# One-hots of two slots per compare, and a four-slot ring that is handed over by pairs

## The chip, the cores and the metric

The kernel runs on one core of a Trainium2 chip. The time is device time in microseconds (us). A core has five engines with their own instruction streams: PE (TensorE, matmuls; its weight loads are listed as PEld), DVE (VectorE), ACT (ScalarE), POOL (GpSimd) and SP (SyncE, which issues most of the DMAs). They meet only at semaphores: an instruction raises one when it is done, and an engine stands at a wait until a semaphore has reached a value.

## The reference

A graph of 6250 nodes with 128 features and 200000 edges that are sorted by destination. Two layers, each added to its input and normalised. What the part under change needs is the sum over a node's edges of the features of the edge's source:

```python
h = node_features @ W + b_W
xi, xj = jnp.split(h, 2, axis=-1)
xji = xj[senders] + (edge_features @ W_e + b_We)
in_degree = jax.ops.segment_sum(jnp.ones_like(receivers), receivers, num_segments=num_nodes)
nodes = xi + jax.ops.segment_sum(xji / (in_degree[receivers] + 1e-06), receivers, num_segments=num_nodes)
x = _layernorm(x + nodes)
...
out = jax.ops.segment_sum(h[src] * norm[:, None], dst, num_segments=N) + b   # second layer, same edges
```

## The kernel before

No row of x is gathered edge by edge. Nodes are cut into NB = 25 blocks of 256 destinations. For each block the kernel counts how often each source node occurs among the edges of each destination (a matrix of counts), and the sum over edges is then a matrix product of x, split in two 16-bit parts, with these counts.

**Counts.** The destinations of a block are taken two by two; eight such windows of up to 128 edges are a *slot*. A block has SL = 16 slots (the last block 7). For a slot VectorE makes two one-hot arrays out of small tables, `lo_oh` (low part of the source's number, 1024 elements per partition) and `key_oh` (high part and which of the two destinations, 800 elements): function `one_hots(b, s)`, lines 594 and 597. TensorE multiplies them, eight matmuls (`count(b, s)`, line 828), and ScalarE copies the result out of PSUM into `counts` (`pair_out`, line 1035).

**The ring.** `lo_oh` and `key_oh` hold RING = 4 slots. VectorE waits before slot number `at` until the semaphore `built` has reached `at + 1 - RING`, that is until slot `at - 4` has been counted. Each slot's second compare raises `hot` by one; TensorE's `count` waits for `hot >= at + 1`. ScalarE's `tables(b)` waits for `hot` too, before it overwrites the tables from two blocks back.

**The order.** Each engine runs a loop over blocks b and slots s that is written out by hand; nothing schedules it. TensorE in block b: at each slot `count(b, s)`, and from slot 1 on a share of `product(b - 1, s)` (lines 846 and 854, the products with the counts of the block before: 98 of them and up to 48 more for the second layer, spread over 15 slots, so 7 to 10 a slot); at slot 1 `messages`, at slot 3 `turn_keys(b + 1)` (line 881), at slots 5 and 11 the edge features' sums `edges` (line 865, 72 matmuls each). VectorE in block b: at each slot `one_hots(b, s)`, and behind it at slot 1 `count_heads` (541), at slot 2 `make_keys(b + 1)` (561 to 581) and `edge_keys(b - 1)` (606), at slot 3 `edge_one_hots(b - 1, 0)` (614) and `z_low` (699), at slot 6 `offset`, at 7 `invert_degrees` and `sums`, at 8 and 9 `count_row` and `start_of`, at 10 the second `edge_one_hots`, at 12 `normalise`. GpSimd's `check_edges` (491 to 494) follows `edge_keys`. Some 700 us in, all blocks are counted; then comes the second layer's gather (line 911), with the counts loaded again, and the normalisation, which use no one-hots.

Of the kernel before, what the change touches and what calls it, by code (L numbers as in the profile page):

```python
# [23 lines left out]
ALU = mybir.AluOpType  # L24
# [3 lines left out]
P = 128  # L28
# [3 lines left out]
NB = -(-N // BN)  # L32
# [3 lines left out]
KW = 2 * HI  # L36
WE = 128
SW = 8
SL = 16
RING = 4  # L40
# [37 lines left out]
def slots(b):  # L78
    return SL if b < NB - 1 else LAST_SLOTS


def first_slot(b):
    return SL * b


def cols(b):
# [60 lines left out]
def reach(engine, sem, value):  # L147


    if not isinstance(value, int) or value > 0:  # L150
        engine.wait_ge(sem, value)
# [43 lines left out]
def layers(nc, block, x, src, dst, ea, W0, b0, We, be, keep, scratch):  # L195
    with ExitStack() as ctx:
# [8 lines left out]
        lo_oh = sb("lo_oh", [P, RING, SW // 2, P, 2], BF16)  # L205
# [10 lines left out]
        key_oh = sb("key_oh", [P, RING, SW // 2, KW, 2], BF16)  # L216
        counter = sb("counter", [P, P, 2], BF16)
# [18 lines left out]
        key_t, lo_t = ([sb(f"{n}{i}", [P, P], BF16) for i in range(2)] for n in ("key_t", "lo_t"))  # L236
# [295 lines left out]
        def _(dve):  # L532
            dv = nc.vector
# [53 lines left out]
            def one_hots(b, s):  # L587
                if s == 0:
                    dve.wait_ge(S["tabled"], b + 1)
                at = first_slot(b) + s  # L590
                reach(dve, S["built"], at + 1 - RING)
                w = slice(SW * s, SW * (s + 1))
                pairs = lambda a: a.rearrange("p (w t) -> p w t", t=2).unsqueeze(2)
                dv.tensor_tensor(lo_oh[:, at % RING, :, :, :],  # L594
                                 counter[:, :, :].unsqueeze(1).to_broadcast([P, SW // 2, P, 2]),
                                 pairs(lo_t[b % 2][:, w]).to_broadcast([P, SW // 2, P, 2]), ALU.is_equal)
                dv.tensor_tensor(key_oh[:, at % RING, :, :, :],  # L597
                                 counter[:, 0:KW, :].unsqueeze(1).to_broadcast([P, SW // 2, KW, 2]),
                                 pairs(key_t[b % 2][:, w]).to_broadcast([P, SW // 2, KW, 2]), ALU.is_equal)\
                  .then_inc(S["hot"], 1)  # L600

            def edge_keys(b):
# [25 lines left out]
            def scales():  # L628
                dve.wait_ge(S["few_out"], 1)
                step(dv.tensor_reduce(out=top[:, :], in_=few_ps[0:1, 0, 0:P], axis=AX.X, op=ALU.max))  # L630
                dv.tensor_scalar(expo[:, :], top[:, :].bitcast(I32), EXP_BITS, None, ALU.bitwise_and)
                few_f = few[:, :].bitcast(F32)
                dv.tensor_scalar(few_f[:, 2:3], top[:, :], ROW_LEAST, None, ALU.mult)
                dv.tensor_scalar(few_f[:, 3:4], top[:, :], X_LEAST, None, ALU.is_ge)
                step(dv.tensor_scalar(sound[:, :], top[:, :], X_MOST, None, ALU.is_le))
                dv.tensor_scalar(few[:, 0:1], expo[:, :], -1.0, float((2 * 127 + X_TOP) * ONE_EXP), ALU.mult, ALU.add)
                dv.tensor_scalar(few[:, 1:2], expo[:, :], -float(X_TOP * ONE_EXP), None, ALU.add)
                step(dv.tensor_tensor(few_f[:, 3:4], few_f[:, 3:4], sound[:, :], ALU.mult))
                dve.sem_inc(S["few_ready"], 1)
# [51 lines left out]
            def normalise(u):  # L691
                dve.wait_ge(S["std_ready"], u + 1)
                dv.reciprocal(std[:, :], std[:, :]).then_inc(S["scale_known"], 1)
# [30 lines left out]
            for b in range(NB + 2):  # L724
                u = b - 2
                for s in range(SL):
                    if b < NB and s < slots(b):
                        one_hots(b, s)
                    if b == 0:
                        if s == 0:  # L730
                            scales()
                        if s == 1:
                            spread_scales()
                        if s == 3:
                            invert_degrees(0)
                    if SL * b + s in LOW_AT:
                        split_low(LOW_AT.index(SL * b + s))
                    if s == 1 and b + 3 < NB:
                        count_heads(b + 3)
                    if s == 2 and b + 1 < NB:  # L740
                        make_keys(b + 1)
                    if b == 1 and s == 6:
                        ready_weights()
                    if s == 2 and 1 <= b < NB:
                        edge_keys(b - 1)
                    if s == 3 and 1 <= b < NB:
                        edge_one_hots(b - 1, 0)
                    if s == (7 if b else 10) and b + 1 < NB:
                        invert_degrees(b + 1)
                    if s == 6 and 0 <= u < NB:  # L750
                        offset(u)
                    if s == 7 and 0 <= u < NB:
                        sums(u)
                    if s == 4 and b == 0:
                        count_row(2)
                    if s == 5 and b == 0:
                        start_of(2)
                    if s == 8 and b + 3 < NB:
                        count_row(b + 3)
                    if s == 9 and b + 3 < NB:  # L760
                        start_of(b + 3)
                    if s == 12 and 0 <= u < NB:
                        normalise(u)
                    if s == (10 if b < NB - 1 else 4) and 1 <= b < NB:
                        edge_one_hots(b - 1, 1)
                    if s == 8 and b == NB - 1:
                        edge_keys(b)
                        edge_one_hots(b, 0)
                    if s == 3 and 1 <= u <= NB:
                        z_low(u - 1)  # L770
# [50 lines left out]
        def _(pe):  # L821
            def count(b, s):
                at = first_slot(b) + s
                pe.wait_ge(S["hot"], at + 1)
                reach(pe, S["pair_out"], at - 1)
                for w in range(SW):
                    half_of, col = w // 4, (w % 4) * KW
                    last = nc.tensor.matmul(pair_ps[at % 2][:, half_of, col:col + KW],  # L828
                                            lo_oh[:, at % RING, w // 2, :, w % 2], key_oh[:, at % RING, w // 2, :, w % 2],
                                            start=True, stop=True)  # L830
                last.then_inc(S["built"], 1)
# [188 lines left out]
        def _(act):  # L1020
# [34 lines left out]
            def tables(b):  # L1055
                act.wait_ge(S["turned"], b + 1)
                if b >= 2:
                    act.wait_ge(S["hot"], first_slot(b - 1))
                a.copy(key_t[b % 2][:, :], keys_ps[:, 0, :])
                a.copy(lo_t[b % 2][:, :], keys_ps[:, 1, :]).then_inc(S["tabled"], 1)  # L1060

# [714 lines left out]
```

## Time and profile before

| | |
|---|---|
| median of 3 runs | 942.07 us (940.08 to 942.12) |
| span of the profiled execution | 940.7 us |
| mean granted TensorE clock | 0.983 of full speed |
| busy: PE, DVE, ACT, POOL | 95%, 74%, 48%, 45% |
| matmuls of `count` (L828) | 3128 |
| compares of `lo_oh`, of `key_oh` | 391 each |

The page gives busy shares for the whole span, which mixes the block loop (to some 700 us) with the second layer (from there on, where VectorE has little to do). Busy times by stretch, the list of waits and the timeline tell the stages apart. A timeline row has the start in us from the span's start, the duration, engine, line, operation, tile written and tiles read, shape, how many instructions are merged into the row, and in brackets how long the engine was idle just before and what ended that.

### The profile page before, as it was taken

What the parts mean: (1) busy time and instruction counts of PE and PEld (TensorE: products, weight loads), DVE (VectorE), ACT (ScalarE), POOL (GpSimd) and SP (SyncE); (2) the same over time, 40 slices, a digit from 0 to 9 for tenths busy, and PEclk for the clock granted to TensorE, in tenths of its full rate; (3) what the DMA queues carried; (4) which work ended last, traced back from release to release, by engine and by line L of the source; (5) the groups of instructions that cost most, each with busy time, mean ns of one, the idle gap of its engine ahead of it and who ended that gap; (6) DMA issues with size and microseconds to landing.
All of it is one profiled execution on the core that took longest, in us unless ns stands there. A gap on an engine that the chain in (4) does not pass through costs nothing.

```text
span 940.7 us, 30861 instructions
## 1 busy us (share of the span) xinstructions
PE 890.2 (95%) x12193; PEld 794.2 (84%) x12193; DVE 695.5 (74%) x1636; ACT 454.9 (48%) x962; POOL 419.3 (45%) x498
## 2 busy tenths in 40 slices
PE   5679999999999999999999999999999999999995
PEld 4667888888988998989999999999988888888864
DVE  5898999999999998898888899888842111112255
ACT  3765665566656665565565556565542000000035
POOL 3347557555764555655565575544332011111100
PEclk9689999999999999999999999999999999999998
DMA  5475888899797987777687777688767887779635
GB/s 164 132 232 212 314 289 293 313 325 315 263 324 286 316 304 236 266 218 248 244 284 249 236 250 211 243 281 258 231 207 305 341 346 285 270 259 324 248 123 165
DMA packets 95727, 244.82 MB, mean 260 GB/s; under 512 B 41194, under 2 KB 63400, under 8 KB 89688
## 3 DMA queue, kind: packets, MB, share of 16 engines
q1 hardware_dynamic: 92312, 237.49, 72.5%
q0 software_dynamic: 2400, 4.88, 1.6%
q8 instruction: 100, 1.64, 0.7%
q10 hardware_dynamic: 864, 0.39, 0.2%
q14 instruction: 51, 0.42, 0.1%
HBM read 183.88 MB, written 58.85 MB: 258 GB/s over the span
## 4 chain that ended last, share of the span: by engine, by line
PE 81%; DVE 10%; issue 3%; ACT 2%; DMA 2%; POOL 0%; ACTq 0%; DVEq 0%
PE x_ps L846 24%; PE pair_ps L911 17%; PE pair_ps L828 13%; PE e_ps L865 10%; PE x_ps L854 9%; DVE key_oh L597 3%; DVE lo_oh L594 3%; PE j_ps L893 2%; DMA early_in<-sums_z 1%; PE pair_ps L920 1%; PE j_ps L894 1%; PE u_vps L1379 1%; ACT counts L1035 1%; DMA xsplit<-in_dst 1%; PE j_ps L943 1%
## 5 line engine op out<-in xcount | busy, mean ns | idle before, releaser
L1035 ACT CAST counts<-pair_ps 128x784 bf16<-128x784 f32 x391 | 315.4, 817 | 256.1 <-PE pair_ps L828 255.3
L846 PE MATMUL x_ps<-counts,xsplit 128*128 128x256 bf16 (+1 forms) x2450 | 306.1, 271 | 1.2 <-issue 1.2
L594 DVE TENSOR_TENSOR lo_oh<-counter,lo_t 128x1024 bf16<-128x1024 bf16 x391 | 274.4, 702 | 41.7 <-PE pair_ps L828 39.8
L846 PEld LDWEIGHTS x_ps<-counts,xsplit 128*128 128x128 f16 x2450 | 221.1, 98 | 31.4 <-issue 9.8
L597 DVE TENSOR_TENSOR key_oh<-counter,key_t 128x800 bf16<-128x800 bf16 x391 | 232.7, 595 | 0.0
L828 PE MATMUL pair_ps<-key_oh,lo_oh 128*128 128x100 bf16 x3128 | 208.5, 209 | 12.9 <-DVE key_oh L597 7.2
L828 PEld LDWEIGHTS pair_ps<-key_oh,lo_oh 128*128 128x128 bf16 x3128 | 182.9, 98 | 27.9 <-DVE key_oh L597 10.9
L865 PE MATMUL e_ps<-streams 128*32 128x128 f32 x3528 | 106.6, 274 | 0.0
L854 PE MATMUL x_ps<-counts,zown 128*128 128x256 bf16 (+1 forms) x840 | 105.9, 269 | 0.6 <-issue 0.6
L911 PE MATMUL pair_ps<-streams,zown 128*128 128x256 bf16 x878 | 99.0, 273 | 0.0
L865 PEld LDWEIGHTS e_ps<-streams 128*32 128x32 f32 x3528 | 93.4, 110 | 4.8 <-issue 1.0
L911 PEld LDWEIGHTS pair_ps<-streams,zown 128*128 128x128 f16 x878 | 85.8, 98 | 11.4 <-issue 0.2
L1184 ACT ACTIVATE xsplit<-xsplit,vec 128x256 f32<-128x256 f32 (+1 forms) x25 | 12.6, 503 | 154.6 <-DVE xsplit L803 154.6
L468 POOL TENSOR_SCALAR bias<-linear,share 128x128 f32<-128x128 f32 x50 | 80.0, 1604 | 14.8 <-DVE vo L680 13.9
L854 PEld LDWEIGHTS x_ps<-counts,zown 128*128 128x128 f16 x840 | 76.1, 97 | 10.9 <-issue 3.4
L911 PE MATMUL pair_ps<-counts,zown 128*128 128x256 bf16 (+1 forms) x732 | 79.9, 269 | 0.0
L911 PEld LDWEIGHTS pair_ps<-counts,zown 128*128 128x128 f16 x732 | 69.3, 98 | 9.2
L436 POOL TENSOR_SCALAR row_f<-cnt 128x1 f32<-128x1 f32 x25 | 14.6, 586 | 121.2 <-DVE head_junk L541 121.1
L614 DVE TENSOR_TENSOR streams<-iota,ekeys 128x1152 f32<-128x1152 f32 x49 | 66.3, 1354 | 0.1
L431 POOL DMA_INDIRECT gsrc<-in_src,start_i x25 | 62.6, 2506 | 7.6 <-issue 7.6
L795 DVE TENSOR_TENSOR s_mem<-pair_ps,early_in 128x256 f32<-128x256 f32 (+1 forms) x23 | 9.6, 418 | 72.6 <-PE pair_ps L911 69.4
L483 POOL TENSOR_TENSOR streams<-streams,key_oh 128x512 bf16<-128x512 bf16 x13 | 15.0, 1150 | 91.0 <-DMA streams<-counts_kept 91.0
(179 smaller groups left out, 881.1 us busy)
## 6 DMA issues: line engine op xcount, KB each, us to landing
streams<-in_edge_attr SPq DMA_DIRECT2D x196, 576.0 KB
counts_kept<-counts SPq DMA_DIRECT2D x10, 1600.0 KB, 9.2
streams<-counts_kept SPq DMA_DIRECT2D x6, 1600.0 KB, 6.5
counts<-counts_kept SPq DMA_DIRECT2D x4, 1600.0 KB, 6.5
counts_kept<-counts SPq DMA_DIRECT2D x2, 3136.0 KB, 12.1
streams<-counts_kept SPq DMA_DIRECT2D x2, 3136.0 KB, 14.6
edst<-in_dst SPq DMA_DIRECT2D x196, 4.5 KB, 1.9
counts<-in_x SPq DMA_DIRECT2D x3, 1024.0 KB, 8.9
```

Source lines behind the costliest of these rows:

```text
L431: g.indirect_dma_start(out=out, out_offset=None, in_=table, in_offset=bass.IndirectOffsetOnAxis(ap=at, axis=0)).then_inc(done, 16)
L468: last = g.tensor_scalar(bias[:, t, :], bje, share[:, 2 * b + t:2 * b + t + 1], None, ALU.mult)
L594: dv.tensor_tensor(lo_oh[:, at % RING, :, :, :], counter[:, :, :].unsqueeze(1).to_broadcast([P, SW // 2, P, 2]), pairs(lo_t[b % 2][:, w]). ...
L597: dv.tensor_tensor(key_oh[:, at % RING, :, :, :], counter[:, 0:KW, :].unsqueeze(1).to_broadcast([P, SW // 2, KW, 2]), pairs(key_t[b % 2][: ...
L614: dv.tensor_tensor(e_oh[g][:, :, :], iota[:, 0:EC].unsqueeze(1).to_broadcast([P, EG * EJ, EC]), ekeys[:, k].unsqueeze(2).to_broadcast([P, ...
L828: last = nc.tensor.matmul(pair_ps[at % 2][:, half_of, col:col + KW], lo_oh[:, at % RING, w // 2, :, w % 2], key_oh[:, at % RING, w // 2, : ...
L846: last = nc.tensor.matmul(x_ps[:, 0, 0:n], xsplit[:, q // 2, q % 2, :], by_hi[:, q // 2, :], start=(q == 0), stop=(q == 2 * HS - 1))
L854: last = nc.tensor.matmul(x_ps[:, 1, 0:n], zsplit[:, z // 2, z % 2, :], by_hi[:, z // 2, :], start=(z == 0), stop=(z == early(k) - 1))
L865: last = nc.tensor.matmul(e_ps[EC * c:EC * (c + 1), g, :], e_oh[g][:, c * EJ + j, :], ebuf[g][:, c, j, :], start=(j == 0), stop=(j == EJ - 1))
L893: nc.tensor.matmul(out, sx[:, t:m:2], wj, start=True, stop=False)
L911: last = nc.tensor.matmul(z_ps[i % 2][:, 0:n], zsplit[:, q // 2, q % 2, :], by_hi[:, q // 2, :], start=(q == early(b)), stop=(q == 2 * HS ...
L1035: a.copy(out.rearrange("p h (g n) -> p h g n", g=2), pair_ps[at % 2][:, :, 0:4 * KW].rearrange("p g (n h) -> p h g n", h=HI)[:, 0:HS]).the ...
```

## The change

One call of `one_hots` makes the one-hots of two slots (of one, where a block has an odd slot left: only the last block's seventh). It is called at even slots. Its two compares have 2048 and 1600 elements per partition. It waits until the later of the two slots that it overwrites has been counted, and raises `hot` once for the pair, so the waits for `hot` count pairs.

```diff
+def hot_pairs(at):
+    return -(-at // 2)
...
             def one_hots(b, s):
                 if s == 0:
                     dve.wait_ge(S["tabled"], b + 1)
-                at = first_slot(b) + s
-                reach(dve, S["built"], at + 1 - RING)
-                w = slice(SW * s, SW * (s + 1))
+                at, n = first_slot(b) + s, min(2, slots(b) - s)
+                reach(dve, S["built"], at + n - RING)
+                w, g = slice(SW * s, SW * (s + n)), SW // 2 * n
+                ring = slice(at % RING, at % RING + n)
                 pairs = lambda a: a.rearrange("p (w t) -> p w t", t=2).unsqueeze(2)
-                dv.tensor_tensor(lo_oh[:, at % RING, :, :, :],
-                                 counter[:, :, :].unsqueeze(1).to_broadcast([P, SW // 2, P, 2]),
-                                 pairs(lo_t[b % 2][:, w]).to_broadcast([P, SW // 2, P, 2]), ALU.is_equal)
-                dv.tensor_tensor(key_oh[:, at % RING, :, :, :],
-                                 counter[:, 0:KW, :].unsqueeze(1).to_broadcast([P, SW // 2, KW, 2]),
-                                 pairs(key_t[b % 2][:, w]).to_broadcast([P, SW // 2, KW, 2]), ALU.is_equal)\
+                dv.tensor_tensor(lo_oh[:, ring, :, :, :].rearrange("p r w k t -> p (r w) k t"),
+                                 counter[:, :, :].unsqueeze(1).to_broadcast([P, g, P, 2]),
+                                 pairs(lo_t[b % 2][:, w]).to_broadcast([P, g, P, 2]), ALU.is_equal)
+                dv.tensor_tensor(key_oh[:, ring, :, :, :].rearrange("p r w k t -> p (r w) k t"),
+                                 counter[:, 0:KW, :].unsqueeze(1).to_broadcast([P, g, KW, 2]),
+                                 pairs(key_t[b % 2][:, w]).to_broadcast([P, g, KW, 2]), ALU.is_equal)\
                   .then_inc(S["hot"], 1)
...
-                    if b < NB and s < slots(b):
+                    if b < NB and s < slots(b) and s % 2 == 0:
                         one_hots(b, s)
...
-                pe.wait_ge(S["hot"], at + 1)
+                pe.wait_ge(S["hot"], hot_pairs(at + 1))
...
-                    act.wait_ge(S["hot"], first_slot(b - 1))
+                    act.wait_ge(S["hot"], hot_pairs(first_slot(b - 1)))
```

VectorE's order in a block of the loop's middle, from slot 2 to slot 5, before. L594 and L597 are a slot's two compares, L561 to L581 `make_keys` (its middle is left out), L606 `edge_keys`, L614 `edge_one_hots`, L699 `z_low`; the brackets name the semaphores waited for:

```order
L594 TENSOR_TENSOR lo_oh<-counter,lo_t 128x1024 [waits built]
L597 TENSOR_TENSOR key_oh<-counter,key_t 128x800
L561 TENSOR_SCALAR bit_i<-gsrc 128x128 [waits turned,window_in0]
...
L606 TENSOR_TENSOR ekeys<-edst,ebase 128x72 [waits e_checked,edge_dst_in0]
L594 TENSOR_TENSOR lo_oh<-counter,lo_t 128x1024 [waits built]
L597 TENSOR_TENSOR key_oh<-counter,key_t 128x800
L614 TENSOR_TENSOR streams<-iota,ekeys 128x1152 [waits e_keyed,e_summed]
L699 SCALAR_TENSOR_TENSOR zown<-x_mem,zscale,zown 128x128 [waits z_high,x1_ready]
L699 SCALAR_TENSOR_TENSOR zown<-x_mem,zscale,zown 128x128
L594 TENSOR_TENSOR lo_oh<-counter,lo_t 128x1024 [waits built]
L597 TENSOR_TENSOR key_oh<-counter,key_t 128x800
L594 TENSOR_TENSOR lo_oh<-counter,lo_t 128x1024 [waits built]
```

The same place after (line numbers have moved by 4 or 5; L599 and L602 are the compares of two slots):

```order
L599 TENSOR_TENSOR lo_oh<-counter,lo_t 128x2048 [waits built]
L602 TENSOR_TENSOR key_oh<-counter,key_t 128x1600
L565 TENSOR_SCALAR bit_i<-gsrc 128x128 [waits turned,window_in0]
...
L611 TENSOR_TENSOR ekeys<-edst,ebase 128x72 [waits e_checked,edge_dst_in0]
L619 TENSOR_TENSOR streams<-iota,ekeys 128x1152 [waits e_keyed,e_summed]
L704 SCALAR_TENSOR_TENSOR zown<-x_mem,zscale,zown 128x128 [waits z_high,x1_ready]
L704 SCALAR_TENSOR_TENSOR zown<-x_mem,zscale,zown 128x128
L599 TENSOR_TENSOR lo_oh<-counter,lo_t 128x2048 [waits built]
L602 TENSOR_TENSOR key_oh<-counter,key_t 128x1600
```

Slot 3's compares have moved from behind `edge_keys` to ahead of `make_keys`, and slot 5's stand in one with slot 4's. Between the pair of slots 2 and 3 and that of slots 4 and 5 now lies all the other work of slots 2 and 3 in one piece.

## Rows read from the trace of the kernel before

**Rows 1.** The page, busy us (share of the span) and instructions of each engine.

```profile
PE 890.2 (95%) x12193; PEld 794.2 (84%) x12193; DVE 695.5 (74%) x1636; ACT 454.9 (48%) x962; POOL 419.3 (45%) x498
```

**Rows 2.** Busy us by stretch: PE, PEld, DVE, ACT, POOL; clock, DMA share, GB/s.

```profile
120.00:160.00 40.00, 37.89 (x658) 33.78 (x659) 40.00 (x93) 23.62 (x47) 23.67 (x26) 1.00 0.81 274
440.00:480.00 40.00, 39.97 (x662) 36.50 (x658) 37.36 (x87) 22.59 (x44) 27.62 (x26) 1.00 0.78 256
```

**Rows 3.** Waits: who waited for whom, us in total, times, longest us.

```profile
POOL row_f L436 <- DVE head_junk L541: 121.1, 23, 8.8
...
DVE lo_oh L594 <- PE pair_ps L828: 39.8, 47, 2.7
...
PE pair_ps L828 <- DVE key_oh L597: 7.2, 10, 1.7
```

**Rows 4.** Timeline of DVE, block 15, from slot 0 to slot 6.

```profile
426.70 0.69 DVE L594 TENSOR_TENSOR lo_oh<-counter,lo_t 128x1024 bf16<-128x1024 bf16 x1 [2.15 <-PE pair_ps L828]
...
429.18 0.31 DVE L541 TENSOR_SCALAR_CACHE_REDUCE head_junk<-heads_sb,th 128x98 bf16<-128x98 f32 x1
...
429.54 0.69 DVE L594 TENSOR_TENSOR lo_oh<-counter,lo_t 128x1024 bf16<-128x1024 bf16 x1
...
430.63 0.22 DVE L561 TENSOR_SCALAR bit_i<-gsrc 128x128 int32<-128x128 int32 x1
...
432.54 0.68 DVE L594 TENSOR_TENSOR lo_oh<-counter,lo_t 128x1024 bf16<-128x1024 bf16 x1
433.14 0.57 DVE L597 TENSOR_TENSOR key_oh<-counter,key_t 128x800 bf16<-128x800 bf16 x1
433.62 1.35 DVE L614 TENSOR_TENSOR streams<-iota,ekeys 128x1152 f32<-128x1152 f32 x1
434.89 0.60 DVE L699 SCALAR_TENSOR_TENSOR zown<-x_mem,zscale,zown 128x128 f16<-128x128 f32 x2
435.42 0.82 DVE L594 TENSOR_TENSOR lo_oh<-counter,lo_t 128x1024 bf16<-128x1024 bf16 x1
...
437.92 0.68 DVE L594 TENSOR_TENSOR lo_oh<-counter,lo_t 128x1024 bf16<-128x1024 bf16 x1
```

**Rows 5.** Timeline of PE: slot 15 of block 14 and slot 4 of block 15.

```profile
430.67 0.53 PE L828 MATMUL pair_ps<-key_oh,lo_oh 128*128 128x100 bf16 x8
...
437.91 0.53 PE L828 MATMUL pair_ps<-key_oh,lo_oh 128*128 128x100 bf16 x8
```

**Rows 6.** Timeline of POOL at the same place: `check_edges`, its first addition.

```profile
435.32 0.37 POOL L492 TENSOR_TENSOR eacc<-eacc,ein 128x72 f32<-128x72 f32 x1
```

**Rows 7.** Timeline, block 4: slot 4's second compare, the next instruction, slot 4's count.

```profile
145.35 0.61 DVE L597 TENSOR_TENSOR key_oh<-counter,key_t 128x800 bf16<-128x800 bf16 x1
145.88 0.82 DVE L594 TENSOR_TENSOR lo_oh<-counter,lo_t 128x1024 bf16<-128x1024 bf16 x1
146.02 0.54 PE L828 MATMUL pair_ps<-key_oh,lo_oh 128*128 128x100 bf16 x8 [0.86 <-DVE key_oh L597]
```

**Rows 8.** Timeline of PE: slot 15 before blocks 3, 7, 10, and slot 4.

```profile
113.17 0.53 PE L828 MATMUL pair_ps<-key_oh,lo_oh 128*128 128x100 bf16 x8
...
120.79 0.54 PE L828 MATMUL pair_ps<-key_oh,lo_oh 128*128 128x100 bf16 x8 [1.20 <-DVE key_oh L597]
...
216.86 0.53 PE L828 MATMUL pair_ps<-key_oh,lo_oh 128*128 128x100 bf16 x8
...
223.45 0.53 PE L828 MATMUL pair_ps<-key_oh,lo_oh 128*128 128x100 bf16 x8
...
294.44 0.88 PE L828 MATMUL pair_ps<-key_oh,lo_oh 128*128 128x100 bf16 x16
...
301.34 0.53 PE L828 MATMUL pair_ps<-key_oh,lo_oh 128*128 128x100 bf16 x8
```

**Rows 9.** Busy us by stretch in block 1, columns as in rows 2.

```profile
63.00:66.00 3.00, 1.41 (x17) 1.08 (x17) 3.00 (x6) 1.02 (x2) 2.79 (x5) 1.00 0.91 393
66.00:70.00 4.00, 3.24 (x35) 2.67 (x39) 3.96 (x8) 1.35 (x4) 1.37 (x3) 0.57 0.79 330
```

## The prediction

> **What bounds the kernel now.** I read the page's engine line first: TensorE is busy 95% of the span, VectorE 74% [rows 1]. That is a mean over stages, so the next view was the busy time by stretch. In 440 to 480 us TensorE is busy 39.97 of 40 us and VectorE 37.4; in 120 to 160 us it is the other way round, VectorE 40.00 and TensorE 37.9 [rows 2]. So the block loop has a front part in which VectorE decides and a long rest in which TensorE does. The list of waits gives the size: in the whole run TensorE's count matmuls (L828) waited for a one-hot ten times, 7.2 us in total, while VectorE waited 47 times, 39.8 us, for a buffer that the counts had not yet freed [rows 3]. So at most 7.2 us can be had by making one-hots sooner, and VectorE has idle time nearly everywhere. What the change can lose is in how that idle time lies: TensorE is fed only because VectorE runs ahead of it into four slot buffers.
>
> **The compares.** In block 15, at slot 3, the compare of the low part takes 0.60 us to the start of the next instruction, that of the keys 0.48 [rows 4]. For 1024 and 800 elements that is 0.536 ns an element and some 0.05 us that doesn't scale. A merged pair of slots therefore costs 2.16 - 2 x 0.05 = 2.06 us instead of 2.16. The 391 slots (24 blocks of 16, the last of 7) become 196 pairs, so VectorE loses about 195 x 0.10 = 20 us of work. The bounds of the saving are 0 and, from the full durations 0.68 and 0.57 in the same rows (slope 0.49 ns, rest 0.18 to 0.19 where they don't overlap), 0.37 us a pair; I take 0.10, since the instructions follow each other here with the overlap that the start times show. This saving reaches the end only where TensorE waited for a one-hot.
>
> A page speaks for the change. The Trainium skill, "VectorE: DVE Perf Modes", section "Rules for kernel authors", says to keep the number of VectorE instructions low, and "Vector Engine (DVE) Microarchitecture Reference", section 5.2, puts about 75 ns on each. By that a pair would cost 2.01 us and the forecast below would be about 2 us lower; the start times here give 50 ns.
>
> **The ring.** This is the term that decides. One-hots have four slot buffers. Before, slot n may be written when slot n-4 has been counted. After, pair (n, n+1) may be written when slot n-3 has been counted, the later of the two it overwrites. And in VectorE's order the second slot of a pair moves ahead of the work that stood between the two: in every block the order at slots 2 to 5 becomes pair (2,3), then make_keys and edge_keys, the edge one-hots, z_low, then pair (4,5). Before, slot 3's compares stood between edge_keys and the edge one-hots.
>
> Follow block 15. TensorE counts slot 15 of block 14 from 430.67 to 431.20 and starts on slot 4 of block 15 at 437.91, 6.71 us later [rows 5]. Pair (2,3) overwrites slots 14 and 15 of block 14, so it can't start before 431.20. (Pair (0,1) is gated by slot 13; VectorE today waits there too, 2.15 us [rows 4], and it and the 0.36 us of count_heads are done in time.) From 431.20 VectorE has to do, before TensorE can start on slot 4:
> - one semaphore step, 0.06 us, and pair (2,3), 2.06;
> - make_keys and edge_keys, 430.63 to 432.54: 1.91 [rows 4];
> - the edge one-hots, 433.62 to 434.89: 1.27 [rows 4];
> - z_low, 434.89 to 435.42: 0.53 [rows 4];
> - pair (4,5), 2.06, and what GpSimd adds. Today the four compares of slots 4 and 5 take 435.42 to 437.92, 2.50 [rows 4], 0.34 over the undisturbed 2.16, and the first of them coincides with GpSimd's L492 [rows 6]. That work follows edge_keys, so it falls on pair (4,5) again. Between 0 and 0.34 I take 0.17;
> - 0.14 from the next instruction's place on VectorE to TensorE's start, as in block 4: 145.88 to 146.02, where TensorE did wait for this compare [rows 7].
>
> Sum: 0.06 + 2.06 + 1.91 + 1.27 + 0.53 + 2.06 + 0.17 + 0.14 = 8.20 us. TensorE is there after 6.71, so it stands 1.49 us. The stall returns each block: the next slot 15 is counted 1.49 later, and so is its chain's start. Nothing hides it, since TensorE is the full engine there and its order is fixed. After slot 4 the other pairs are in time: pair (6,7) follows (4,5) at once and is used two slots and 2.1 us of edges later; continued in the same way, the walk has pair (10,11) and the second edge one-hots done over 1 us before TensorE wants them.
>
> On GpSimd's share a page and a row differ. The row shows 0.82 for a compare that takes 0.68 elsewhere, so 0.14 for an overlap of 0.27 us (L492 from 435.32, 0.37 long) [rows 4, 6]. The Trainium skill, "SBUF — State Buffer", section "SBUF: two separate sides", has the two engines share a port as an exclusive lock for a whole instruction. By that pair (4,5) would wait 0.3 to 0.7 us and the sum would be 3 to 12 us higher; the trace shows half an overlap, and I go by it.
>
> **The other blocks.** What a block gains in length is 8.20 minus its time from the end of slot 15 to the start of slot 4 today, whatever stall that time already holds. The 12 blocks 12 to 23 have ten products a slot and look like block 15: 12 x 1.49 = 17.9. Blocks 8 to 11 have nine: in block 10 it is 294.97 (0.53 into a row of 16) to 301.34, 6.37 [rows 8], so 4 x 1.83 = 7.3. Blocks 6 and 7, eight: 217.39 to 223.45, 6.06 [rows 8], 2 x 2.14 = 4.3. Blocks 3 to 5 are like block 3: 113.70 to 120.79, 7.09, of which 1.20 is already a wait for the one-hot [rows 8]: 3 x 1.11 = 3.3. Block 2 has block 3's products without its wait, 5.89: 2.3. Block 1 has today two waits at slots 3 and 4 and no z_low; its chain comes out within 0.3 us, taken as 0.2. In block 0 the first count waits for two slots instead of one, 2.06 - 1.08, about 1.0, and scales() moves by as much. Block 24 has no make_keys and edge work before slot 4: 0. Smaller waits for one-hots in blocks 2 to 5, some 0.8 us of the 7.2, go: -0.8.
>
> Total: 17.9 + 7.3 + 4.3 + 3.3 + 2.3 + 0.2 + 1.0 - 0.8 = 35.5 us. Hidden at no cost: count_heads, sums, count_row and start_of come up to one pair later, and their users (GpSimd's row_of, ScalarE's root, the gathers for two blocks on) have several us; deg_known comes some 2.6 us later for GpSimd, which waits 121 us for count_heads alone today [rows 3]. ScalarE's tables(b) waits for the same one-hots as before, counted in pairs. The second phase from 700 us on has no one-hots and only moves.
>
> The profiled execution has a span of 940.7 us; the median of the three runs is 942.07, 1.4 above. 942.1 + 35.5 = 977.6, rounded to 977.
>
> **Rivals.**
> 1. *Faster: the ring still covers.* If pair (4,5) came within 6.7 us of slot 15's count, only the saving would be left, and TensorE would get back what it waited for VectorE, at most 7.2 us [rows 3]: 935. For it speaks VectorE's large idle time. It decides where the chain drops below TensorE's 6.71 us; for that 1.5 us of 8.20 must go, and the largest saving per pair that a row allows, 0.37, takes 2 x 0.27. I give it 5%. It is also what the rule on instruction counts would give.
> 2. *Nothing to see.* The saving in the front part and stalls of 0.2 to 0.3 us a block cancel: 942. 3%.
> 3. *Half the stall.* Compares cheaper than I take them (2 x 0.27) and no GpSimd share, so a chain of 7.5: 0.7 less in each of the 22 blocks 2 to 23, 15 us off, 962. 9%.
> 4. *The clock falls too.* In block 1 TensorE stood twice for one-hots, was busy 1.41 of 3.0 us, and the granted clock was 0.57 in the next 4 us, the lower of its two levels (1.2 instead of 2.4 GHz) for most of it [rows 9]. That costs up to 4 x 0.43 = 1.7 us. A single wait of 1.20 in block 3 had no such fall. The new stalls are 1.5 to 2.3 us. Falls in blocks 2, 6 and 7 alone add 5 us, inside my range; in all 22 blocks 37 us: 1015. 8% for more than a third of the blocks.
> 5. *The change doesn't do what it says*, the merged compare running at a lower rate than two: each 1 us on a pair would add 2 us to every chain, near 1020. Shape and types are the same but for the count of groups. 2%.
>
> **How the numbers follow.** My case has 73%. Its range is set by the chain: without GpSimd's share and with 0.15 less a pair it is 7.7 us, 11 us less over the 22 blocks; without any saving and with all of 0.34 it is 8.57, 8 more; blocks 0 to 2 may add or take 2. So 966 to 988, which leaves out rivals 1 to 3 and most of 4 and 5. A difference of 0.3%, 2.8 us, is about what a measurement of this kernel can tell from none. Faster by more: 5%. Within: 3%. Slower by more: 92%.
>
> **What the changed profile would show.** TensorE's L828 waiting for key_oh some 23 times, once a block at slot 4, 35 to 40 us in total instead of 7.2; VectorE waiting for L828 at about three places a block; blocks 15 to 23 with a period 1.5 us longer; a merged low compare of about 1.15 us and a merged key compare of 0.91 to the next start; the granted clock at 1.00 through the loop. I am wrong if L828's waits stay under 15 us, if they lie at other slots than 4, or if the merged compares take other than 2.0 to 2.2 us together.

## The result and the profile after

The changed kernel takes 990.37 us (median of 6 runs, 989.92 to 993.55) beside 942.1 us of the kernel before on the same chip: ratio 1.051, 95% interval 1.0483 to 1.0537. The forecast was 977 us with a range of 966 to 988. Sign, place and mechanism of the main loss came as forecast; the time is 13 us above the forecast and 2.4 us above the range, because two losses beside it had no term in the sum. The profiled execution has a span of 988.0 us, 47.3 more than the 940.7 before, and it is these 47.3 us that are accounted for below.

The page of after, busy us by engine; it answers to [rows 1]:

```profile
PE 896.9 (91%) x12193; PEld 794.2 (80%) x12193; DVE 674.0 (68%) x1246; ACT 453.4 (46%) x962; POOL 428.3 (43%) x498
```

VectorE has 390 instructions and 21.5 us of work less, and TensorE the same instructions and a smaller share. The saving is real and buys nothing. The waits of after (us in total, times, longest), to be read beside [rows 3]:

```profile
POOL row_f L440 <- DVE head_junk L545: 176.3, 23, 11.5
...
DVE lo_oh L599 <- PE pair_ps L833: 103.9, 65, 3.9
...
PE pair_ps L833 <- DVE key_oh L602: 44.4, 29, 2.5
```

TensorE waits 44.4 us for one-hots instead of 7.2, VectorE 103.9 us for a free buffer instead of 39.8: each engine waits for the other in turn. By stretch (columns as in [rows 2]) TensorE has lost its full 40 us in the steady part, and in the front part the clock is no longer 1.00:

```profile
120.00:160.00 40.00, 35.12 (x540) 30.68 (x539) 34.27 (x61) 19.23 (x40) 27.11 (x31) 0.91 0.78 270
440.00:480.00 40.00, 38.50 (x604) 34.85 (x605) 33.63 (x60) 21.85 (x43) 22.44 (x26) 1.00 0.81 264
```

**The chain in one block.** This is the timeline of after from slot 15 of block 15 to slot 4 of block 16, the block after the one of [rows 4] and [rows 5]. First TensorE, then VectorE.

```profile
458.65 0.53 PE L833 MATMUL pair_ps<-key_oh,lo_oh 128*128 128x100 bf16 x8
...
467.52 0.54 PE L833 MATMUL pair_ps<-key_oh,lo_oh 128*128 128x100 bf16 x8 [1.47 <-DVE key_oh L602]
```

```profile
459.21 1.23 DVE L599 TENSOR_TENSOR lo_oh<-counter,lo_t 128x2048 bf16<-128x2048 bf16 x1 [0.71 <-PE pair_ps L833]
460.36 0.98 DVE L602 TENSOR_TENSOR key_oh<-counter,key_t 128x1600 bf16<-128x1600 bf16 x1
461.26 0.22 DVE L565 TENSOR_SCALAR bit_i<-gsrc 128x128 int32<-128x128 int32 x1
...
463.02 0.23 DVE L611 TENSOR_TENSOR ekeys<-edst,ebase 128x72 f32<-128x72 int32 x1
463.35 1.36 DVE L619 TENSOR_TENSOR streams<-iota,ekeys 128x1152 f32<-128x1152 f32 x1
464.63 0.61 DVE L704 SCALAR_TENSOR_TENSOR zown<-x_mem,zscale,zown 128x128 f16<-128x128 f32 x2
465.15 1.36 DVE L599 TENSOR_TENSOR lo_oh<-counter,lo_t 128x2048 bf16<-128x2048 bf16 x1
466.44 1.02 DVE L602 TENSOR_TENSOR key_oh<-counter,key_t 128x1600 bf16<-128x1600 bf16 x1
467.38 1.35 DVE L599 TENSOR_TENSOR lo_oh<-counter,lo_t 128x2048 bf16<-128x2048 bf16 x1
```

Slot 15 is counted at 459.18. VectorE, idle 0.71 us for just that, starts pair (2,3) at 459.21 and works without a pause until pair (4,5) is done; TensorE starts slot 4 at 467.52. That is 8.34 us, forecast 8.20. Before, TensorE took 6.71 [rows 5], so the block grows by 1.63 us, and it does so in each of blocks 12 to 22.

**Where the 47.3 us are**, by comparing the start of each slot's count matmuls in the two traces, from one slot to the next:
- slot 4 of blocks 2 to 23: 37.7 us;
- slots 5 and 6 of blocks 3, 4 and 7, right behind that stall, at the lower clock: 4.7 us;
- slots 8 to 12 of seven blocks (4, 11, 12, 18, 19, 21, 22), where TensorE waits for no one-hot: 6.5 us;
- gone: 0.8 us of small waits at slot 11 of blocks 2, 3 and 5, and 1.1 us of other gaps that the trace of before has in blocks 5, 6 and 9;
- blocks 0 and 1 together: 0.1 us.

That makes 47.1; the rest is rounding and the part behind the loop.

### The profile page after: what moved, and what is told of

The parts are those of the page before. It is cut to its first block, busy times and chain, and to the rows that moved or that the text cites. A ratio compares the mean times of both kernels' runs of the same rounds, so it can differ in the third digit from the quotient of the medians.

```text
span 988.0 us, 30471 instructions
## 1 busy us (share of the span) xinstructions
PE 896.9 (91%) x12193; PEld 794.2 (80%) x12193; DVE 674.0 (68%) x1246; ACT 453.4 (46%) x962; POOL 428.3 (43%) x498
## 3 DMA queue, kind: packets, MB, share of 16 engines
q8 instruction: 100, 1.64, 0.7%
## 4 chain that ended last, share of the span: by engine, by line
PE 70%; DVE 16%; issue 8%; DMA 2%; ACT 2%; POOL 0%; DVEq 0%; ACTq 0%
PE x_ps L851 19%; PE pair_ps L916 16%; PE pair_ps L833 12%; PE e_ps L870 11%; PE x_ps L859 8%; DVE key_oh L602 5%; DVE lo_oh L599 4%; DMA early_in<-sums_z 1%; PE pair_ps L925 1%; DVE zown L704 1%; PE u_vps L1384 1%; ACT counts L1040 1%; PE j_ps L948 1%; DMA rows<-in_dst,row_i 1%; PE e_ps L878 1%
## 5 line engine op out<-in xcount | busy, mean ns | idle before, releaser
L599 DVE TENSOR_TENSOR lo_oh<-counter,lo_t 128x2048 bf16<-128x2048 bf16 x196 | 248.2, 1267 | 105.8 <-PE pair_ps L833 103.9
L833 PE MATMUL pair_ps<-key_oh,lo_oh 128*128 128x100 bf16 x3128 | 208.8, 209 | 52.3 <-DVE key_oh L602 44.4
L602 DVE TENSOR_TENSOR key_oh<-counter,key_t 128x1600 bf16<-128x1600 bf16 x196 | 200.9, 1025 | 0.0
L870 PE MATMUL e_ps<-streams 128*32 128x128 f32 x3528 | 109.2, 278 | 0.7 <-issue 0.7
L870 PEld LDWEIGHTS e_ps<-streams 128*32 128x32 f32 x3528 | 95.4, 112 | 6.3 <-issue 1.9
L472 POOL TENSOR_SCALAR bias<-linear,share 128x128 f32<-128x128 f32 x50 | 70.9, 1425 | 11.9 <-DVE vo L685 10.9
L808 DVE TENSOR_TENSOR xsplit<-pair_ps,dinv_row 128x256 f32<-128x256 f32 (+1 forms) x25 | 10.5, 419 | 58.2 <-PE pair_ps L925 57.0
```

The source lines that it names most:

```text
L472: last = g.tensor_scalar(bias[:, t, :], bje, share[:, 2 * b + t:2 * b + t + 1], None, ALU.mult)
L599: dv.tensor_tensor(lo_oh[:, ring, :, :, :].rearrange("p r w k t -> p (r w) k t"), counter[:, :, :].unsqueeze(1).to_broadcast([P, g, P, 2]) ...
L602: dv.tensor_tensor(key_oh[:, ring, :, :, :].rearrange("p r w k t -> p (r w) k t"), counter[:, 0:KW, :].unsqueeze(1).to_broadcast([P, g, KW ...
L870: last = nc.tensor.matmul(e_ps[EC * c:EC * (c + 1), g, :], e_oh[g][:, c * EJ + j, :], ebuf[g][:, c, j, :], start=(j == 0), stop=(j == EJ - 1))
```

## The experiments

Theory A is that of the forecast: pairs over four buffers make VectorE wait for slot 15, and everything between pair (2,3) and pair (4,5) then lies on TensorE's path. Theory B: the merged compare itself is slow. Theory C, formed on the result: the stalls also bring the clock down, which multiplies them. Each kernel was run beside the kernel before (medians 942.3 to 943.0 us); "increment" is what a block gains at slot 4 over the kernel before.

### One part of the change at a time

All three have single compares, one slot each. The first only waits by pairs for the ring:

```
-                reach(dve, S["built"], at + 1 - RING)
+                if s % 2 == 0:
+                    reach(dve, S["built"], at + min(2, slots(b) - s) - RING)
```

> One slot per compare and the old order; only the wait for the ring is by pairs (at even slots, for both slots that are overwritten). Theory A (the new stall is a chain on VectorE that starts when slot 15 is counted: ring wait, order and hand-over by pairs make it long): the chain to slot 4 has one slot's compares less ahead of slot 4 than in the changed kernel, 0.06 + 1.08 + 1.91 + 1.08 + 1.27 + 0.53 + 1.08 + 0.17 + 0.14 = 7.3 us against TensorE's 6.71, so 0.6 us a block at slot 4 and more in the blocks with fewer products: about 956 us (950 to 962). Theory B (the merged compares themselves cost, by their length or by what they block): 942 us.

Measured: 962.73 us, ratio 1.0221 (1.018 to 1.0263). The increment is 0.77 us in blocks 14 to 21, 0.8 to 1.5 in blocks 7 to 13.

The second only has the order of pairs:

```
-                    if b < NB and s < slots(b):
-                        one_hots(b, s)
+                    if b < NB and s < slots(b) and s % 2 == 0:
+                        for k in range(s, min(s + 2, slots(b))):
+                            one_hots(b, k)
```

> One slot per compare, ring wait and hand-over slot by slot; only the order is that of the changed kernel (the compares of slots s and s+1 in a row, the other work behind both). Theory A: only slot 3's compares wait for slot 15, so the chain is 0.06 + 1.08 + 1.91 + 1.27 + 0.53 + 1.08 + 0.17 + 0.14 = 6.2 us, under 6.71: no stall at slot 4 in the blocks with ten products, 942 us (939 to 947). Theory B: 942 us too.

Measured: 945.49 us, ratio 1.0047 (1.0025 to 1.0069). No increment in blocks 12 to 23.

The third has both edits, which is the kernel after without the merging and with one hand-over a slot:

> One slot per compare, with the order and the ring wait of the changed kernel; what is left out of the change is the merging and the hand-over by pairs (TensorE may take slot 4 before slot 5 is made). Theory A: 0.06 + 2.16 + 1.91 + 1.27 + 0.53 + 1.08 + 0.17 + 0.14 = 7.3 us, 0.6 us a block: 956 us (950 to 962); the 1.0 us a block from here to the changed kernel's 8.34 is slot 5's share of pair (4,5). Theory B: 942 us, all of the loss being in the merged compares.

Measured: 967.99 us, ratio 1.0271 (1.0243 to 1.0299); increment 0.82 in blocks 14 to 22. The waits of TensorE for one-hots in the three, in this order:

```profile
PE pair_ps L829 <- DVE key_oh L598: 25.4, 28, 1.7
```
```profile
PE pair_ps L829 <- DVE key_oh L597: 7.1, 8, 1.8
```
```profile
PE pair_ps L830 <- DVE key_oh L598: 23.8, 24, 1.8
```

What follows: waiting by pairs makes a stall by itself, the order by itself costs 2.5 us of time and nothing in blocks 12 to 23. Wait and order give half of the increment of 1.63. I put the other half down to the hand-over, which no run has by itself: with single compares TensorE may start slot 4 when slot 4's one-hots are there, a merged pair is handed over only with slot 5's, about 1 us later, less what merging saves. Both kernels came out above their expected 956, since I had put down only the steady blocks' increment: blocks 7 to 13 grow by up to 1.5 us, and each trace has some 3 to 5 us of gaps at slots 9 to 12 with no wait for VectorE.

### More buffers

The kernel after with six buffers. The third pair's low parts lie in an unused tail of `streams`, its keys in a new tile; a few small tiles share space to make room.

```
-RING = 4
+RING = 6
+KEPT = 4
...
+        key_more = sb("key_more", [P, RING - KEPT, SW // 2, KW, 2], BF16)
```

> The changed kernel with six slot buffers instead of four (the third pair lies in memory that is free in the block loop; a few small tiles share memory for it). Pair (2,3) then waits for slot 13, about 3 us sooner, while merging, order and hand-over by pairs stay. Theory A: the chain reaches slot 4 after some 5.3 us, no stall, TensorE's waits for one-hots fall below 7 us, time 934 to 942. Theory B: the merged compares cost the same as in the changed kernel, 980 to 990 us. Theory C (beyond the chain, clock falls and unexplained gaps in TensorE's stream add some 9 us of their own): if they follow from the stalls they are gone here, if not the time stays some us above 942.

Measured: 940.09 us, ratio 0.996 (0.9937 to 0.9983). No increment in blocks 7 to 23, and TensorE waits for one-hots about as long as before the change:

```profile
PE pair_ps L843 <- DVE key_oh L612: 8.1, 7, 2.5
```

So merged compares cost nothing by themselves and theory B falls; in after, too, a pair's two compares take 1.15 + 0.90 = 2.05 us to the next start (459.21, 460.36 and 461.26 above), forecast 2.06. This kernel is faster than both, by 0.4% over the one before.

### The chain made shorter and longer

Four buffers and pairs as in after; edge_keys and the first edge one-hots are moved ahead of pair (0,1), z_low behind pair (4,5). The first line makes edge_keys wait until VectorE's own earlier edge one-hots are done:

```
+                reach(dve, S["e_hot"], edge_group(b, 0))
...
+                    if s == 0 and 1 <= b < NB:
+                        edge_keys(b - 1)
+                        edge_one_hots(b - 1, 0)
                     if b < NB and s < slots(b) and s % 2 == 0:
                         one_hots(b, s)
...
-                    if s == 3 and 1 <= u <= NB:
+                    if s == 5 and 1 <= u <= NB:
                         z_low(u - 1)
```

> The kernel after, four buffers and pairs as they are; only the work that stands on VectorE between pair (2,3) and pair (4,5) is thinned: edge_keys and the first edge one-hots stand before pair (0,1), z_low behind pair (4,5). Theory A (the stall at slot 4 is the chain from slot 15's count, 8.34 us, minus TensorE's 6.71): the chain loses 1.27 + 0.4 + 0.53 us and is 6.1 to 6.4, below 6.71, so the wait at slot 4 is gone in blocks 12 to 23 and the time is 938 to 948, with some stalls left in blocks 3 to 11. Rival (pairs over four buffers cost a stall wherever the other work stands): 965 to 990.

Measured: 941.47 us, ratio 0.9989 (0.9969 to 1.0009). The increment is 0.00 in blocks 10 to 23. The chain now reads (timeline of VectorE, one block):

```profile
456.06 1.23 DVE L599 TENSOR_TENSOR lo_oh<-counter,lo_t 128x2048 bf16<-128x2048 bf16 x1 [0.71 <-PE pair_ps L833]
...
458.10 0.22 DVE L565 TENSOR_SCALAR bit_i<-gsrc 128x128 int32<-128x128 int32 x1
...
459.86 1.23 DVE L599 TENSOR_TENSOR lo_oh<-counter,lo_t 128x2048 bf16<-128x2048 bf16 x1
461.01 0.98 DVE L602 TENSOR_TENSOR key_oh<-counter,key_t 128x1600 bf16<-128x1600 bf16 x1
461.91 0.60 DVE L705 SCALAR_TENSOR_TENSOR zown<-x_mem,zscale,zown 128x128 f16<-128x128 f32 x2
```

Pair (4,5) is done 5.85 us after pair (2,3) starts (456.06 to 461.91), under TensorE's 6.71. This takes the whole loss back with only the order changed and that wait added, so the loss was the chain.

The opposite: the first edge one-hots of each block written twice, the second time after a wait for the first.

```
-                        edge_one_hots(b - 1, 0)
+                        edge_one_hots(b - 1, 0, 2)
```

> The kernel after, with the first edge one-hots of each block written twice, so that the chain to slot 4 is longer by one compare, 1.27 us, and one wait for itself, about 0.1. Theory A (every us on the chain is a us of the block): +1.4 us in blocks 2 to 23, 30 us, so 1017 to 1024. Theory C (longer waits bring the granted clock down after most of them, at 1.5 us each): in 22 blocks up to 33 us more, 1030 to 1055. If the time stays under 1005, the chain isn't what TensorE waits for.

Measured: 1048.77 us, ratio 1.113 (1.1112 to 1.1149). The increment is 3.12 us in blocks 12 to 22 (3.35 in block 14), 1.49 more than in after: theory A's term. It makes 69.9 us over blocks 2 to 23 instead of 37.7. Another 29.9 us lie at slots 5 and 6, where after has 4.7: the granted clock falls at 17 of these 22 stalls. One of them, by stretch (columns as in [rows 2]):

```profile
450.00:475.00 25.00, 21.18 (x301) 18.77 (x299) 20.23 (x34) 13.50 (x28) 12.86 (x13) 0.99 0.54 185
474.70:478.10 3.40, 3.40 (x38) 2.70 (x39) 3.19 (x7) 1.90 (x4) 1.13 (x4) 0.50 1.16 215
480.00:505.00 25.00, 24.47 (x342) 21.77 (x337) 16.31 (x30) 14.14 (x28) 8.32 (x12) 1.00 0.67 227
```

So theory A and theory C both hold: a us on the chain is a us of the block, and a stall of 3 us or more costs 1.4 to 1.7 us more in most blocks.

### After, a second time

> The kernel after, unchanged, for a second trace. Theory A: the wait at slot 4 is 1.4 to 1.6 us in blocks 12 to 23 again, and the time is 988 to 994. The falls of the granted clock (blocks 3, 4, 7 in the first trace, 4.7 us) and the gaps of TensorE at slots 8 to 12 (about 6 us in the first trace, in blocks 4, 11, 12, 18, 22) lie in the same blocks if the program's order makes them, and elsewhere if they are chance.

Measured: 986.52 us (984.85 to 993.03), ratio 1.0494 (1.0454 to 1.0534); span of this trace 982.8. Slot 4 of blocks 2 to 23 gives 37.7 us, as in the first trace. The clock falls again behind block 3 and block 4 and this time not in block 7 (3.1 us). The gaps at slots 8 to 12 are in part elsewhere (blocks 3, 13 and 14; blocks 4 and 21 have them again; 4.6 us, net of what is gone 1.9). So the stall at slot 4 is fixed by the program; which blocks have gaps and falls of the clock is partly chance. The two traces differ mainly by these, and by 1.2 us in blocks 0 and 1.

### One slot a compare over six buffers

The edit of the six buffers, in the kernel before. It was to part what six buffers gave from what merging gave.

> The kernel before, with six buffers instead of four, one slot a compare as before. It parts what six buffers gave in the pairs' kernel (940.1) from what merging gave. If the one wait that six buffers take away is that of TensorE for one-hots (7.2 us in all before, 2 to 4 of them in blocks 3 to 6), it comes out at 938 to 941, the same as the pairs; if merging gave the gain, at 942 to 944.

Measured: 963.21 us, ratio 1.022 (1.0167 to 1.0273). Both expectations failed. TensorE waits hardly at all for one-hots (4.0 us), but in blocks 10 to 21 slot 6 is 0.9 to 1.7 us late, 14 us in all, since the edge matmuls of slot 5 (72, before 2.17 us) stop in the middle. Timeline of TensorE, then of GpSimd:

```profile
450.68 1.85 PE L877 MATMUL e_ps<-streams 128*32 128x128 f32 x48
452.86 0.89 PE L877 MATMUL e_ps<-streams 128*32 128x128 f32 x24 [0.33 <-issue]
```
```profile
450.79 1.15 POOL L442 DMA_INDIRECT gdst<-in_dst,start_i  x1 [0.27 <-issue]
452.25 3.78 POOL L442 DMA_INDIRECT gsrc<-in_src,start_i  x1 [0.31 <-issue]
```

GpSimd's gathers for a later block wait, through its `shares`, for invert_degrees on VectorE. With six buffers VectorE runs further ahead, and the gathers start 0.1 us into the edges. In the kernel before they start some 0.8 us after the edges, in the six-buffer kernel of pairs mostly 1.2 to 1.9 us after their start. That made theory D: the gathers disturb the edges. The test moves invert_degrees on VectorE:

```
-                    if s == (7 if b else 10) and b + 1 < NB:
+                    if s == 10 and b + 1 < NB:
                         invert_degrees(b + 1)
```

> The kernel with six buffers and one slot a compare (963.2 us), with invert_degrees of the next block moved on VectorE from slot 7 to slot 10. GpSimd's share, and behind it its gathers for a later block, wait for invert_degrees; in that kernel they start in the first us of TensorE's edge matmuls of slot 5, and these took 3.0 us instead of 2.2 in blocks 10 to 21, 1.1 us a block. In the kernel before, the gathers start 0.8 us after the edges end. Theory D (the gathers' start slows the edge matmuls): moved by some 3 us, the gathers come after the edges and the 1.1 us are gone in 12 blocks: 944 to 952. Rival (one slot a compare over six buffers delays something else at slot 5): 958 to 966.

Measured: 959.07 us, ratio 1.0161 (1.0129 to 1.0193). The disturbance is gone: blocks 12 to 22 are as long as in the kernel before, to within 0.07 us, and the idle time inside the edge matmuls (view of that line) falls from the first of these rows to the second:

```profile
  issue: 24.0, 58
```
```profile
  issue: 5.2, 14
```

But the time hardly moved, because the gathers are now late. In blocks 3, 6 and 11 VectorE's make_keys waits for them, and each of these blocks is 6.3 to 6.5 us longer:

```profile
DVE bit_i L572 <- DMA gsrc<-in_src,start_i: 27.7, 5, 7.6
```

So theory D holds as to the coincidence, and a new wait took the gain. Why a gather's start slows those matmuls the trace doesn't say. In blocks 12 to 22 three kernels agree: singles over four buffers, singles over six with this move, and pairs over six. Merging gives the steady part nothing and takes nothing from it.

### Both cures together

Six buffers and the short chain.

> Six buffers, pairs, and the short chain (edge_keys and the first edge one-hots ahead of pair (0,1), z_low behind pair (4,5)). Six buffers alone left TensorE 8 us of waits for one-hots, all in blocks 1 to 6; the short chain alone (four buffers) left 5.8. Theory A: no stall is left in blocks 7 to 23, and the front part may give 2 to 5 us: 934 to 940. If the front part is bound by VectorE's whole work, as its 100% busy share at 120 to 160 us says, the order does nothing: 938 to 942.

Measured: 942.94 us, ratio 1.0006 (0.999 to 1.0022). No gain over six buffers alone, and no better than before. The forecast for theory A missed, but not at the one-hots: slot 4 of blocks 3 to 6 is 3.5 us earlier than in the kernel before (2.5 with six buffers alone), and the 6.1 us of waits that are left lie in blocks 0 and 1. What took the gain is slot 6, which comes 0.2 to 0.6 us late in each of blocks 11 to 22, 3.6 us in all. GpSimd's gathers now start next to the edge matmuls of slot 5, and these take 2.4 to 2.8 us instead of 2.17, theory D's loss in a smaller size. Block 15, TensorE and GpSimd:

```profile
439.34 2.40 PE L881 MATMUL e_ps<-streams 128*32 128x128 f32 x72
```
```profile
438.95 1.46 POOL L446 DMA_INDIRECT gdst<-in_dst,start_i  x1 [0.27 <-issue]
440.72 1.37 POOL L446 DMA_INDIRECT gsrc<-in_src,start_i  x1 [0.30 <-issue]
```

## Why the prediction was right and where it was not

**Right: what decides, and where.** The stall is at slot 4, once a block, from slot 15's count through pair (2,3), make_keys, edge_keys, edge one-hots, z_low and pair (4,5). Shortening that list took the loss away, lengthening it by one compare raised it by 1.49 us a block. TensorE waited 29 times, 44.4 us, where some 23 times and 35 to 40 us were forecast. The saving of 0.10 us a pair is what the trace shows (2.05 against 2.16), and it reaches nothing, as forecast. Rivals 1, 2, 3 and 5 are out: the ring doesn't cover (44.4 us of waits), the increment isn't half, and the compare isn't slow.

**Right, partly by luck: the price of a shared moment with GpSimd.** Pair (4,5) took 2.23 us from 465.15 to 467.38, the 2.06 + 0.17 of the sum, while three GpSimd instructions ran beside it:

```profile
465.05 0.38 POOL L496 TENSOR_TENSOR eacc<-eacc,ein 128x72 f32<-128x72 f32 x1
465.52 1.24 POOL L497 TENSOR_SCALAR ein<-ekeys 128x72 f32<-128x72 f32 x1
466.84 0.81 POOL L498 TENSOR_TENSOR eacc<-eacc,ein 128x72 f32<-128x72 f32 x1
```

The 0.17 was the middle of 0 to 0.34, and nothing in the rows of before chose it. GpSimd paid more than VectorE: the last two of these took 0.71 and 0.40 us in block 15 of the kernel before. The Trainium skill, "SBUF — State Buffer", section "SBUF: two separate sides", has such instructions of the two engines exclude each other from start to end; by the prediction's estimate from that it would have been 2.36 us or more, so the trace doesn't agree here. The Trainium skill, "Vector Engine (DVE) Microarchitecture Reference", section 5.2, gives about 75 ns for an instruction; the two instructions saved per pair gave 0.11 us together, 55 ns each.

**Mis-sized by 0.18 us a block: make_keys and edge_keys.** I took 1.91 us from [rows 4], and it was 2.09 (461.26 to 463.35). The difference is behind edge_keys: it is 0.33 us from its start to the edge one-hots, before it was 0.15 to the next compare, at 432.54 [rows 4]:

```profile
432.39 0.22 DVE L606 TENSOR_TENSOR ekeys<-edst,ebase 128x72 f32<-128x72 int32 x1
```

Before, slot 3's compares stood between the two, so the edge one-hots found their keys ready; now they stand right behind the instruction whose semaphore they wait for. The change moves the cover away, and I priced the steps one by one as if the order between them didn't matter. Against it stand 0.04 us of small overestimates; the chain is 8.34 instead of 8.20. Over the blocks this gives 37.7 us where the sum had 35.1.

**Wrong: rival 4 was a matter of yes or no.** I gave the falling clock 8% as a case of its own and left it out of the forecast, though the text says that falls in blocks 2, 6 and 7 would add 5 us. It fell in blocks 3, 4 and 7 and added 4.7. It belonged into the sum: the trace of before shows a fall in block 1 [rows 9], and from the sum, with the waits that were there already, stalls of 1.8 to 2.3 us followed for blocks 2 to 7. The rows after block 3's stall and after block 7's (columns as in [rows 2]):

```profile
121.00:124.40 3.40, 0.96 (x15) 0.66 (x13) 3.40 (x6) 0.90 (x2) 3.08 (x6) 1.00 0.33 90
124.40:127.80 3.40, 3.40 (x44) 2.77 (x45) 3.38 (x7) 1.96 (x4) 1.92 (x4) 0.50 1.00 218
127.80:131.20 3.40, 3.40 (x77) 3.04 (x70) 1.94 (x6) 0.26 (x1) 2.83 (x3) 0.99 0.60 234
205.00:208.40 3.40, 1.30 (x17) 0.96 (x16) 3.40 (x4) 1.32 (x3) 3.15 (x4) 1.00 0.22 43
234.00:237.10 3.10, 1.40 (x20) 1.32 (x21) 3.10 (x4) 0.82 (x2) 1.75 (x2) 0.99 0.30 71
237.10:240.50 3.40, 3.40 (x65) 3.04 (x65) 3.38 (x7) 1.14 (x3) 1.78 (x4) 0.50 1.06 206
```

In the second row TensorE is busy all the time at 0.50, the lower level of 1.2 GHz; in the third the clock is back. The fourth row is block 6: a stall of 2.11 us, as long as block 7's, and no fall. "The clock at 1.00 through the loop" was wrong for three stretches.

**Wrong: no term for what comes and goes.** The sum put the gaps at slots 8 to 12 at nothing; they are 6.5 us in the first trace and 4.6 in the second. All but those at slot 12 follow a signal of TensorE that arrives late (last section). In blocks 2 to 23 the trace of before has one such signal that is over 0.6 us late, each trace of after eight, so the change may bring them; by what step isn't shown. The trace of before also has two gaps of the kind at slot 12, 0.57 and 1.24 us in blocks 5 and 6, which I had not looked at, since they lie far from any wait on VectorE. The gaps are part of why single executions of after lie between 985 and 994 us. The range had 2 us for "blocks 0 to 2" and nothing for this.

**Blocks 0 and 1** were put at 1.2 us and gave 0.1. The small waits for one-hots that go gave the 0.8 us forecast. In sum 35.5 became 37.7 + 4.7 + 6.5 - 0.8 - 1.1 + 0.1 = 47.1: the chain was 2.6 us short, the clock 4.7 and the gaps, net, 5.4 us that the sum left out, and blocks 0 and 1 were 1.1 too much. The forecast itself, 977, was 977.6 rounded down.

## What to carry to other kernels

Merging two steps of a producer doubles the grain of a ring: the producer must wait for two consumed buffers and the consumer for two filled ones, so the same four buffers hold only two pairs. Before merging, write down the producer's work between one such wait and the next hand-over and compare it with the consumer's time for the same stretch: here 8.34 against 6.71 us, and moving 2.1 us of other work out of that stretch, or two more buffers, each took the whole loss back. A stall that returns in every block should be priced with the clock that it can take along, as part of the sum and not as a rival.

## What the runs showed of the hardware

**TensorE seems to stop where a transfer of its program comes late.** The trace of after has 100 transfers of 16 KB on the queue that the page calls instruction, 1.64 MB in all. In block 6 TensorE stops between the second and the third product of slot 12, with everything there that it needs; this is the timeline of after, and the kernel before does the same at the same matmul (1.24 us at 213.48):

```profile
222.11 0.38 PE L851 MATMUL x_ps<-counts,xsplit 128*128 128x256 bf16 x2
223.45 0.83 PE L851 MATMUL x_ps<-counts,xsplit 128*128 128x256 bf16 x6 [0.96 <-issue]
```

The instruction transfer before it ran from 221.03 to 222.04, so TensorE resumed 1.41 us after its end; in the kernel before it ran from 211.10 to 212.12, 1.36 us before the resumption. Seven of the ten kernels of the experiments stop at this same matmul too. Most other places of this kind lie multiples of 256 of TensorE's recorded instructions (to one) away from it. With places and transfers matched in order, TensorE reaches no place earlier than 1.24 us after the end of its transfer, in any of the twelve traces; that it waits for the transfer is inferred from these times. The transfers start up to some 8 us after TensorE has passed a place about 280 recorded instructions earlier (2 to 3 us in the middle), so it seems that they queue with the data transfers; that was not tested. Of the gaps at slots 8 to 12 in the two traces of after, those at slot 12 (blocks 22 and 13, 1.1 and 1.0 us) are of this kind.

**A signal can arrive late.** ScalarE mostly starts to copy a count within 0.1 us of its end. In the first trace of after, at slots 6 and 7, it starts 1.2 to 2.7 us late in exactly the seven blocks with gaps at slots 8 to 12. This is block 12 (TensorE, ScalarE, VectorE):

```profile
383.20 0.53 PE L833 MATMUL pair_ps<-key_oh,lo_oh 128*128 128x100 bf16 x8
...
387.18 0.52 PE L833 MATMUL pair_ps<-key_oh,lo_oh 128*128 128x100 bf16 x8 [0.91 <-ACT counts L1040]
```
```profile
386.22 1.53 ACT L1040 CAST counts<-pair_ps 128x784 bf16<-128x784 f32 x2 [5.32 <-PE pair_ps L833]
```
```profile
386.40 1.23 DVE L599 TENSOR_TENSOR lo_oh<-counter,lo_t 128x2048 bf16<-128x2048 bf16 x1 [2.50 <-PE pair_ps L833]
```

Slot 6 is counted at 383.73 and slot 7 at 385.18, but ScalarE copies both from 386.22 on, and VectorE, which waits for slot 7, starts at 386.40. So it is TensorE's signal that is late for both, and TensorE then stands at slot 8 for the copy (in blocks 18 and 22 it also stops 0.71 and 0.43 us within the products before). In both traces of after, a gather of GpSimd starts within 1.3 us of the end of each such count, and where the gathers were moved later (the test of theory D) the late copies lie at slots 8 to 15. But most blocks have a gather at the same place and no late signal, so the cause stays open.

**Clock.** Behind single stalls of 2.1 to 2.4 us the granted clock fell to its lower level in three of the five blocks 3 to 7 in one trace of after and in two in the other; it did not in block 1, behind 2.5 us, nor behind the 17 stalls of 1.5 to 1.9 us. With the longer chain it fell at 17 of 22 stalls of 3.0 to 3.8 us. One fall cost 1.5 to 1.6 us in after, 1.76 on average with the longer chain.

**A gather's start and matmuls of many small instructions.** With one slot a compare over six buffers the 72 edge matmuls of blocks 10 to 21 took 3.1 to 3.8 us instead of 2.2, a gather of GpSimd starting within their first microsecond; the products between, ten in 1.25 us, showed nothing of the kind in the same blocks. The start alone doesn't decide: in block 14 of the six-buffer kernel of pairs a gather starts 0.4 us into the edges, and they take 2.17 us.
